# Three-piece bf16 splits: the last subtraction writes the third piece itself, and its copy goes

## The reference

```python
h = jnp.maximum(_layernorm(x, axis=-1), 0.0)
# layer 2, over row = src and col = dst
w = inv_sqrt(deg_out)[row] * inv_sqrt(deg_in)[col]
agg_fwd = segment_sum(w[:, None] * h[col], row, n)
agg_bwd = segment_sum(w[:, None] * h[row], col, n)
x = x + 0.5 * (agg_fwd @ W_src.T + b_src) + 0.5 * (agg_bwd @ W_dst.T + b_dst)
# layer 3
ssum = segment_sum(edge_weight[:, None] * h[src], dst, n)
agg = ssum / maximum(cnt, 1)[:, None]
x = x + relu(layernorm(h + agg @ W_rel.T + b_rel + h @ W_root.T) * gamma + beta)
```

## Time and profile before

| | |
|---|---|
| median of 3 runs | 8532.7 us (8531.45 to 8534.68) |
| profiled execution, its own time | 8540.75 us |
| span of its records | 8538.9 us |
| TensorE matmul busy | 6832.8 us (80%) |
| VectorE busy | 6298.4 us (74%) |
| ScalarE busy | 3141.4 us (37%) |
| GpSimd busy | 4335.6 us (51%) |

### The profile page before, as it was taken

One profiled execution on the slowest core, in us unless ns is written; L12 is line 12 of the kernel. 1 busy time (PEld: TensorE's weight loads), 2 busy tenths in 40 slices (PEclk: granted clock), 3 DMA queues, 4 the chain that ended last, 5 costly groups with the idle time before them and its releaser, 6 DMA issues. The chain is left out here.

```text
span 8538.9 us, 219666 instructions
## 1 busy us (share of the span) xinstructions
PE 6832.8 (80%) x59894; PEld 5740.4 (67%) x60293; DVE 6298.4 (74%) x20368; ACT 3141.4 (37%) x8821; POOL 4335.6 (51%) x5493
## 2 busy tenths in 40 slices
PE   5865577789968888888886997884997884997887
PEld 4764466655556666666665777774996774897775
DVE  7999888832257777777776777776887776887777
ACT  3533322233323333333323551001660004668991
POOL 0000377400047777777752556774667771566770
PEclk8985689999977787878778999998999995999996
DMA  0000266510024444444433886777886763887772
GB/s 23 2 2 1 72 140 139 139 53 30 30 72 107 104 107 107 106 107 107 106 96 139 287 288 213 208 207 143 330 338 204 208 201 120 319 338 214 208 207 92
DMA packets 636888, 1262.19 MB, mean 148 GB/s; under 512 B 117598, under 2 KB 175621, under 8 KB 636385
## 3 DMA queue, kind: packets, MB, share of 16 engines
q1 hardware_dynamic: 415409, 704.46, 25.1%
q0 software_dynamic: 199040, 544.46, 23.6%
q10 hardware_dynamic: 22196, 10.20, 0.4%
HBM read 780.96 MB, written 477.75 MB: 147 GB/s over the span
## 5 line engine op out<-in xcount | busy, mean ns | idle before, releaser
L1177 POOL DMA_INDIRECT GS<-t1d,KI x1564 | 1486.8, 951 | 1293.8 <-POOLq L141 814.9
L1069 PE MATMUL PS<-w,AREA 128*128 128x128 f32 x6048 | 810.1, 283 | 158.8 <-DVE w L971 63.9
L1069 PE MATMUL PS<-w,GS 128*128 128x128 f32 x6128 | 796.4, 283 | 173.0 <-DVE AREA L1014 76.9
L1069 PEld LDWEIGHTS PS<-w,GS 128*128 128x128 f32 x6128 | 728.7, 193 | 241.0 <-DVE w L971 163.2
L1069 PEld LDWEIGHTS PS<-w,AREA 128*128 128x128 f32 x6048 | 722.4, 191 | 246.6 <-DVE w L971 137.5
L971 DVE TENSOR_TENSOR w<-PS,KI 128x512 f32<-128x512 f32 x964 | 666.8, 692 | 300.1 <-issue 283.4
L2484 PE MATMUL PS<-AREA 128*128 128x128 bf16 x13392 | 841.1, 219 | 20.9 <-ACT GS L2410 4.7
L2484 PEld LDWEIGHTS PS<-AREA 128*128 128x128 bf16 x13392 | 790.0, 98 | 77.1 <-POOL AREA L2428 9.1
L2459 DVE TENSOR_SCALAR AREA<-PS,w 128x1024 bf16<-128x1024 bf16 x558 | 716.0, 1284 | 156.8 <-PE PS L2470 78.5
L2428 POOL TENSOR_TENSOR AREA<-AREA,w 128x192 int32<-128x192 int32 x1116 | 529.5, 506 | 468.1 <-PE PS L2484 291.9
L2410 ACT ACTIVATE GS<-PS 128x1024 f32<-128x1024 f32 x558 | 571.7, 1025 | 310.5 <-PE PS L2484 298.9
(11 more groups left out here) (428 smaller groups left out, 14099.7 us busy)
## 6 DMA issues: line engine op xcount, KB each, us to landing
xbuf<-GS SPq DMA_DIRECT2D x558, 512.0 KB
XR<-in_edge_attr SPq DMA_DIRECT2D x780, 256.0 KB
pbuf<-AREA SPq DMA_DIRECT2D x482, 256.0 KB
GS<-t1d,KI POOLq DMA_INDIRECT x1564
AREA<-t2d ACTq DMA_DIRECT2D x121, 64.0 KB
GS<-xbuf,KI POOLq DMA_INDIRECT x484
keyd<-AREA POOLq DMA_INDIRECT x482
AREA<-xbuf,KI POOLq DMA_INDIRECT x480
```

The costliest lines, as they stand in the source:

```text
L1069: i = e.matmul(PS[:, s % 3, 0:128], feats(s)[0:m, r, 0:D], SELW[s % 3][0:m, width * r:width * r + 128], start=(r == 0), stop=(r == 3))
L1177: e.indirect_dma_start(GS[0:m, s, r, 0:wide], None, table, bass.IndirectOffsetOnAxis(ap=idx[0:m, c:c + 1].bitcast(U32), axis=0)).then_inc( ...
```

## The change

At each of the three places the second subtraction writes its result as bf16 into the place of the third piece, and the copy that did so is dropped. The number of pieces and their values stay: r - p1 is rounded to bf16 when it is written.

In `p_cells` two of six casts go, and two of four subtractions write bf16 numbers 12 bytes apart where they wrote an f32 table. In `produce_q` ScalarE writes two pieces for each group, and what raised `pc[2]` is now the second subtraction on VectorE, `sb_[1]`: the buffer's next load, GpSimd's start and TensorE's start wait for that. In `produce_p` the chunk's fifth GpSimd instruction goes, and `tb` is raised by the fourth.

```diff
@@ p_cells, vector
-                for i in range(3):
+                for i in range(2):
                     if k:
                         e.wait_ge(wp, k)
                     e.tensor_copy(fv[:, :, a + i], v).then_inc(wp, 1)
-                    k += 1
-                    if i < 2:
-                        e.wait_ge(wp, k)
-                        e.tensor_tensor(v, v, fv[:, :, a + i], ALU.subtract).then_inc(wp, 1)
-                        k += 1
+                    e.wait_ge(wp, k + 1)
+                    e.tensor_tensor(v if i == 0 else fv[:, :, a + 2], v, fv[:, :, a + i], ALU.subtract).then_inc(wp, 1)
+                    k += 2
@@ produce_q, sync
                 if k >= 4:
-                    e.wait_ge(pc[2], k - 3)
+                    e.wait_ge(sb_[1], k - 3)
@@ produce_q, scalar
-            for k in range(len(groups) + 2):
-                for i in range(3):
+            for k in range(len(groups) + 1):
+                for i in range(2):
                     piece(k - i, i)
@@ produce_q, gpsimd (before its loop), and the same line in tensor
-            e.wait_ge(pc[2], len(groups))
+            e.wait_ge(sb_[1], len(groups))
@@ produce_q, vector
-                    e.tensor_tensor(v, v, tv[:, w_:w_ + m, i, :], ALU.subtract).then_inc(sb_[i], 1)
+                    o = v if i == 0 else tv[:, w_:w_ + m, 2, :]
+                    e.tensor_tensor(o, v, tv[:, w_:w_ + m, i, :], ALU.subtract).then_inc(sb_[i], 1)
@@ produce_p, split
-            e.tensor_tensor(TS[i], TS[i], out_[:, 1, :], ALU.subtract).then_inc(sem_, 1)
-            e.wait_ge(sem_, n0 + 4)
+            return e.tensor_tensor(out_[:, 2, :], TS[i], out_[:, 1, :], ALU.subtract)
@@ produce_p, gpsimd
-                    split(e, i, pc, ck * 4, TPC[i])
-                    e.tensor_tensor(TPC[i][:, 2, :], TS[i], zero, ALU.add).then_inc(tb, 1)
+                    split(e, i, pc, ck * 3, TPC[i]).then_inc(tb, 1)
```

More of the change, by code:

```diff
@@ L2364, in produce_q @@
         tl = [p.sem(f"tl{i}") for i in range(4)]
-        pc, sb_ = [p.sem(f"pc{i}") for i in range(3)], [p.sem(f"sb{i}") for i in range(2)]
+        pc, sb_ = [p.sem(f"pc{i}") for i in range(2)], [p.sem(f"sb{i}") for i in range(2)]
         ra, rb, kb, oh, gm, ev, rz = (p.sem(k) for k in ("ra", "rb", "kb", "oh", "gm", "ev", "rz"))
@@ L2596, in unit @@
                     e.wait_ge(gl, n * 16)
-                    split(e, 0, pc, n * 4 - 4, TPC[0])
-                    e.tensor_tensor(TPC[0][:, 2, :], TS[0], zero, ALU.add).then_inc(tb, 1)
+                    split(e, 0, pc, n * 3 - 3, TPC[0]).then_inc(tb, 1)
                 units(e, unit)
```

## The result

The changed kernel takes 8490.1 us in the median of four runs (8489.6 to 8494.2) against 8532.5 of the kernel before: 42.4 us less, a ratio of 0.9951 (95% interval 0.9934 to 0.9968). The forecast was 8487. Its profiled execution has a span of 8488.8 us against 8538.9, which is more than the medians differ, since the one of before stood 8 us above its own median.

A forecast was written before the change was run, and what follows sets the result against it. The prediction took staging to be bound by a buffer's turn and the chunk loop by close chains, GpSimd's split ruling. Staging 29.5, chunk loop 12, fields 4 and first split 0.5 made 46 us, from 8532.7 to 8487; range 8465 to 8507.

The forecast's parts named there:

- Staging: Two stagings of produce_q: a shorter buffer turn takes rounds from 2.17 to 1.54 us and saves 29.5 us.
- the case that was feared: Staging: denser loads take 0.5 us longer, a round is 1.71 us and the gain 11.5 us each (23).
- The lower bound: Staging: rounds no faster than VectorE's two subtractions, 1.29 us, which gives 5 us more each (40 in all).
- the removed copies are not the gain as such; the shorter turn is: Staging in produce_q: the gain comes from a buffer's shorter turn, 29.5 us over two stagings.
- The second rival: Staging: loads are bound by transfer, rounds stay near 2.2 us, some 19 us go in all, 8514; chance 0.10.
- Chunk loop: Loop of produce_p: dropping the fifth GpSimd instruction takes a chunk from 3.90 to 3.80 us, saving 12 us.
- the 3.7 that the prediction gave to ScalarE's own work: Chunk loop of produce_p: ScalarE's own work from one table load to the next needs 3.7 us a chunk.
- The first rival: Chunk loop of produce_p gives nothing, as list, ScalarE's issues or stores rule; 34 us go, 8499; chance 0.18.
- The sign that was set for it: Chunk loop: if waits for the list of rows, 18.2 us before, double, the first rival holds.
- Fields: p_cells: two casts go (5.7 us), two strided-writing subtractions cost 0.8 us more each; saves 4 us (3.7 to 5.7).
- the most is the whole surcharge of a strided write: Fields in p_cells: a subtraction writing 12 bytes apart costs at most 1.0 us more, taken from the cast.
- Sum: Whole kernel: 29.5 + 12 + 4, and 0.5 for the first chunk's split, make 46 us saved, leaving 8487.

The follow-up runs named there:

- after_six: The change with six staging buffers in place of four; 8477.6 us, ratio 0.9936 to the kernel before.
- before_six: The kernel before, all three ScalarE copies kept, with six staging buffers in place of four; 8503.9 us, ratio 0.997 to the kernel before.
- lists_early: The change with the list of rows of chunk ck+2 loaded one block earlier, table load unmoved; 8481.2 us, ratio 0.9941 to the kernel before.
- chunks_only: The kernel before with only the produce_p part of the change; 6.1 us less, ratio 0.9994 to the kernel before.
- the second group: One of three groups of follow-up runs, each timed against the kernel before in its own group; that kernel took 8530 us in this one.
- change_again: The change once more, unaltered, in the same group as all_three; 10159.0 us, ratio 0.9961 to the kernel before.
- all_three: The change with six staging buffers, the earlier list of rows, and the fields' third piece cast by ScalarE; 10129.9 us against 10199.1 before, ratio 0.9934.

## Why the prediction was right, and where not

**Staging, 29.5 forecast, 13.9 and 14.7 measured.** The mechanism and the size were right: a round of 1.54 us was forecast, 4.76 / 3 = 1.59 came, and 38.5 us a staging became 38.8 and 39.2. The picks behind it took 0.5 and 1.4 us more than before, which is why the phases show 13.4 and 13.3. From a load's issue to the round that it lets begin pass 2.8 us in the mean (2.7 before), where the sum had 2.67 from a single row; (1.96 + 2.8) / 3 is the 1.59 that came. So the case that was feared, loads 0.5 us longer, did not come. The lower bound was set wrongly: VectorE at 1.29 a round was to give 5 us more each, but with nothing to wait for it takes 1.20 a round and a staging falls to 30.6 (`after_six`), 8 more. The step that "the removed copies are not the gain as such; the shorter turn is" is shown by `before_six`: two more buffers give as much as the change with all copies left. The second rival, transfers as the bound, is refuted by the changed kernel's own 164 GB/s and the 162 of `after_six`, where the kernel before had 119.

**Chunk loop, 12 forecast (3.80 us a chunk), 9.8 in the phase (3.82).** That several chains lay close together was right, and so was the one that took over: the list of rows. What was not foreseen is how regular it is: two chunks of about 3.6 us and then one of about 4.2, in turn through most of the loop; why is open. The chunk of 3.71 in `lists_early` lies at the 3.7 that the prediction gave to ScalarE's own work, but that it is ScalarE's floor is not shown: ScalarE's L2618 still waits there for TensorE 222 times, 136.3 us in all, and TensorE is busy 94.4 of 100 us. The first rival, nothing from this loop, is refuted by the phase, but only by the phase: `chunks_only` as a whole is not told from before. The sign that was set for it, waits for the list that double, misled: at the products they nearly tripled (6.7 to 19.5 us), and the phase still fell by 9.8.

**Fields, 4 forecast, nothing measured.** This step failed: "the most is the whole surcharge of a strided write", taken from the cast as 1.0 us. The cast's row was the wrong neighbour: its dense form takes 0.98, not the 1.79 that I put there from a two-operand pass, so its own surcharge is 1.8, and the subtraction's is 3.6. The rows from the trace of before had no dense cast of this length and no two-operand instruction with a strided result, and a bound between two forms is none for a third. So the new subtraction took 5.38 us and not 3.0, and ate the cast's 2.83. Why the subtraction pays twice what the cast pays is open. The rule of the Trainium skill (Vector Engine (DVE) Microarchitecture Reference, "The SBUF access granule: adjacent pairs"), by which all three streams hopping cost 1.98 ns a column, was measured on whole words and does not hold here: 5.39 / 1573 = 3.43 ns with the result alone hopping 12 bytes. The worst row of that table of the Trainium skill, 2.5 ns for a result stepping 24 words, is passed too.

**Sum.** 46 forecast; the touched phases gave 36.4, the median 42.4. The three parts alone give 36.8 in phases and 37.1 by their medians. Nothing ties the rest of the 42 to the change: over the profiles of the second group and the first pair, the last phase, which no kernel here alters, lasted 201 to 207 us in no order with the edits, and the interval of the change itself reaches about 14 us to either side. But `change_again` too gained 2 us more than its touched phases, so a small gain elsewhere is not ruled out. What makes the untouched phases vary is open; no run looked at it. That 8487 came within 3 us of 8490 is luck: with the terms as they came out the sum gives 8496.

## What to carry to other kernels

When an instruction is dropped from a pipelined stage, ask which ring's turn it shortened: here the copies had time to spare, and two more buffers bought the same 28 us in the stagings; only with them did the dropped copies show their own 17. Where several chains of one loop lie within a few per cent, an edit to one earns little until the next is moved too (here 10 us and 3 to 6 us alone, 24 together). And before folding a conversion into an arithmetic instruction, look at how the result lies: in runs of 128 numbers the subtraction cost no more than before (0.68 us), with single numbers 12 bytes apart it cost all that the copy had cost.

## What the runs showed of the hardware

A VectorE subtraction of 1573 numbers a partition takes 1.80 us with a dense result, and 1.91, 3.65 and 5.39 with bf16 results 4, 8 and 12 bytes apart: 1.1 ns a number more for each 4 bytes beyond the first 4. ScalarE's copy into the 12-byte table takes 5.44 (`all_three`), within 1% of that, so the price is not VectorE's alone. VectorE's cast pays half of that, 2.78. A strided bf16 operand adds only 0.44, and nothing where the result is 8 or 12 bytes apart already. GpSimd's subtraction takes 0.427 us with a bf16 result of 128x128, as with f32 (0.428).
